# Cross attention in a decoder layer: units placed elsewhere in the order of the tensor engine, and the maximum products in pairs of 64 contraction rows

## What is computed

```
kv_r   = rope(kv_c)                                # [32, 1444, 64]
scores = q_r . k_r        over 16 heads            # 1600 query rows x 1444 keys
attn   = softmax(scores, axis=-1)
ctx_c  = attn @ kv_r                               # 64 numbers for each query row
out    = (ctx_c through w_kc_kv and Wo)            # [32, 100, 256]
x      = x + out
```

## Time and profile before

| | |
|---|---|
| median of 3 runs | 2818.99 us (2817.58 to 2822.96) |
| profiled execution, first to last instruction (span) | 2817.1 us |
| PE busy in the span | 2649.9 us (94%) |
| DVE busy | 2034.9 us (72%) |
| POOL busy | 1512.6 us (54%) |
| ACT busy | 1026.2 us (36%) |
| granted clock of PE, mean | 0.971 of full |

### The profile page before, as it was taken

The page is one execution under the profiler, slowest core; times in us unless marked ns, Lnnn a source line. Parts: engine busy times, 40 slices in busy tenths (PEclk is TensorE's granted clock), DMA queues, the critical chain, the costliest instruction groups (busy, mean ns, idle before and its releaser), DMA issues. The chain is left out here.

```text
span 2817.1 us, 40800 instructions
## 1 busy us (share of the span) xinstructions
PE 2649.9 (94%) x13650; PEld 1632.3 (58%) x13650; DVE 2034.9 (72%) x3271; ACT 1026.2 (36%) x1537; POOL 1512.6 (54%) x438
## 2 busy tenths in 40 slices
PE   6999769999979999999999999999999999999598
PEld 4545457767635555555555555555555555555388
DVE  6888758888776777677767776777677767775475
ACT  3223221111114444444444444444444444444143
POOL 1544500000026776777677767776777677767421
PEclk9999879999969999999999999999999999999799
DMA  4000031212111001100010011001100010000011
GB/s 120 19 17 23 12 107 43 47 41 47 40 41 32 21 20 25 35 20 20 25 35 20 20 25 35 20 20 25 35 20 20 25 35 20 20 20 6 25 41 41
DMA packets 56196, 88.97 MB, mean 32 GB/s; under 512 B 7146, under 2 KB 47166, under 8 KB 56016
## 3 DMA queue, kind: packets, MB, share of 16 engines
q1 hardware_dynamic: 56144, 88.29, 12.3%
HBM read 65.13 MB, written 23.14 MB: 31 GB/s over the span
## 5 line engine op out<-in xcount | busy, mean ns | idle before, releaser
L1376 POOL TENSOR_TENSOR x_acc<-x_acc,x_prob 120x1600 f32<-120x1600 f32 (+1 forms) x320 | 1157.1, 3616 | 281.7 <-ACT x_prob L1392 277.9
L1485 DVE TENSOR_REDUCE x_mx<-x_ring 124x1 f32<-124x480 f32 (+3 forms) x1248 | 784.4, 658 | 424.6 <-PE x_ring L1595 424.0
L1392 ACT ACTIVATE x_prob<-x_scores 120x800 f32<-120x800 f32 (+1 forms) x768 | 633.1, 839 | 920.2 <-PE x_scores L1542 913.4
L1554 PE MATMUL x_context<-x_prob,x_kv 120*64 120x400 f32 (+1 forms) x3072 | 653.5, 519 | 0.0
L1539 PE MATMUL x_scores<-x_qa,x_ka 128*120 128x400 f32 (+1 forms) x1536 | 552.3, 360 | 0.0
L1542 PE MATMUL x_scores<-x_qb,x_kb 128*120 128x400 f32 (+1 forms) x1536 | 530.7, 345 | 0.0
L1595 PE MATMUL x_ring<-x_ka,x_qa 128*124 128x480 f32 (+3 forms) x1248 | 516.7, 437 | 3.2 <-DVE x_mx L1485 1.1
L1595 PEld LDWEIGHTS x_ring<-x_ka,x_qa 128*124 128x124 f32 (+1 forms) x1248 | 220.0, 186 | 321.7 <-issue 161.2
L1539 PEld LDWEIGHTS x_scores<-x_qa,x_ka 128*120 128x120 f32 (+1 forms) x1536 | 280.0, 182 | 107.4 <-issue 60.6
L1554 PEld LDWEIGHTS x_context<-x_prob,x_kv 120*64 120x64 f32 (+1 forms) x3072 | 166.8, 135 | 227.0 <-issue 162.7
L1542 PEld LDWEIGHTS x_scores<-x_qb,x_kb 128*120 128x120 f32 (+1 forms) x1536 | 280.0, 182 | 26.4 <-DMA x_qb<-scratch_m 0.2
(11 more groups left out here) (165 smaller groups left out, 2867.8 us busy)
## 6 DMA issues: line engine op xcount, KB each, us to landing
x_qraw<-scratch_qp SPq DMA_DIRECT2D x64, 400.0 KB, 5.2
scratch_qp<-q_qs SPq DMA_DIRECT2D x32, 400.0 KB, 3.8
x_raw<-in_ctx SPq DMA_DIRECT2D x32, 360.0 KB
a_x<-in_x SPq DMA_DIRECT2D x8, 400.0 KB
scratch_x<-a_x SPq DMA_DIRECT2D x8, 400.0 KB
q_x<-scratch_x SPq DMA_DIRECT2D x8, 400.0 KB
x_xr<-scratch_x SPq DMA_DIRECT2D x32, 100.0 KB
scratch_x<-x_x SPq DMA_DIRECT2D x32, 100.0 KB
```

Source lines behind the costliest of these rows:

```text
L1376: pool.tensor_tensor(acc[0:rows, parity], first, prob[0:rows, c % PR], ALU.add).then_inc(acc_done.sem, 1)
L1392: act.activation(prob[0:rows, c % PR, u * HALF:(u + 1) * HALF].rearrange("p (j s) -> p j s", j=2), psc[0:rows, u, :, 0:BANK], ACT.Exp).the ...
L1485: dve.tensor_reduce(mx[0:block_rows(r), r, i:i + 1], ring[0:block_rows(r), bank, 0:b - a], AX.X, ALU.max).then_inc(rg.read[bank], 1)
L1554: mm = pe.matmul(pav[DC * s:DC * s + DC, j, 0:BANK], kv[0:rows, parity, c], prob[0:rows, c % PR, cols], start=c == 0, stop=c == LC - 1)
```

## The change

The order of the units in `side` is another one, and engines take their parts at other places:

- `kvT` goes to chunk 0 (two) and chunk 1 (one); `out` to chunk 1 behind the last score; the two `den` to the ends of chunks 4 and 5. The maxima stand in pairs behind pieces 1, 3 and 5, in chunks 2 to 9: six, six, four, four, four, four, six and five.
- Two maxima of a pair are products over 64 contraction rows each: one of partitions 0 to 63 of `qa` and `ka`, the other of partitions 64 to 127 of `qa` and `kb`. For that `kb` and `qb` keep the data that they had in their lower half in their upper half, and the row of ones or maxima is row 0. The maximum is now taken over products with the high part of the key alone.
- `den` is copied by ACT to SBUF (`save_den`); DVE takes the reciprocal from there in four halves in chunks 5 to 8 (`invert`); the products with the context (`normalise`) are one in chunk 10 and one in chunk 11.
- `rope` is taken by DVE at chunk 11 of the slot before, behind the first and ahead of the second `normalise`; ACT copies `kv_high` at the very start of the slot, ahead of the exponentials of chunk 0; DVE makes `kv_low` at the start of the slot (`split_kv`).

```diff
-        for place, u in (((1, 3), ("kvT", 0)), ((2, 0), ("kvT", 1)), ((2, 3), ("kvT", 2)), ((C_M, 2), ("mT",)),
-                         ((C_M, 3), ("den", 0)), ((C_M, 5), ("den", 1)), ((0, 4), ("out",))):
+        for place, u in (((0, 1), ("kvT", 0)), ((0, 3), ("kvT", 1)), ((1, 1), ("kvT", 2)), ((1, 3), ("out",)),
+                         ((C_M, 2), ("mT",)), ((4, 5), ("den", 0)), ((5, 5), ("den", 1))):
             side[place].append(u)
-        ticks = [(c, i) for c in range(3, C_M) for i in range(PIECES) for _ in range(1 + (ORDER[i][0] == "context"))]
-        for m in range(3 * MB):
-            side[ticks[m * len(ticks) // (3 * MB)]].append(("max", m // 3, m % 3))
+        maxima = iter([("max", m // 3, m % 3) for m in range(3 * MB)])
+        for c, at_pieces in ((2, (1, 1, 3, 3, 5, 5)), (3, (1, 1, 3, 3, 5, 5)), (4, (1, 1, 3, 3)), (5, (1, 1, 3, 3)),
+                             (6, (1, 1, 3, 3)), (7, (1, 1, 3, 3)), (8, (1, 1, 3, 3, 5, 5)), (9, (1, 1, 3, 3, 5))):
+            for i in at_pieces:
+                side[c, i].append(next(maxima))
...
-                act.copy(kb[0:DC, parity, a:b], ring[0:DC, bank, 0:b - a]).then_inc(rg.read[bank], 1)
+                act.copy(kb[DC:P, parity, a:b], ring[0:DC, bank, 0:b - a]).then_inc(rg.read[bank], 1)
+
+            def save_den(n, j):
+                wait(act, ctx_normed.sem, ctx_normed.at(n - 1, j + 1))
+                bank, value = rg.place(n, ("den", j))
+                act.wait_ge(rg.filled[bank], value)
+                act.copy(dens[:, j], ring[:, bank, 0:BANK]).then_inc(rg.read[bank], 1)
...
             def slot(n, parity, more):
+                if more:
+                    act.wait_ge(kv_roped.sem, kv_roped.at(n, 1))
+                    bank, value = rg.place(n - 1, ("kvT", 2))
+                    wait(act, rg.filled[bank], value)
+                    act.copy(ks[:, :, 0:DC].bitcast(F32R), rotated[:]).then_inc(kv_high.sem, 1)
                 for c in range(LC):
...
-                        if 2 * c + u in (3, 4, 5) and more:
-                            copy_turned(n, 1 - parity, 2 * c + u - 3)
+                        if 2 * c + u in (0, 1, 2) and more:
+                            copy_turned(n, 1 - parity, 2 * c + u)
+                        if (c, u) in ((4, 1), (5, 1)):
+                            save_den(n, c - 4)
...
+            def invert(n, j, half):
+                bank, value = rg.place(n, ("den", j))
+                dve.wait_ge(rg.read[bank], value)
+                cols = slice(half * (BANK // 2), (half + 1) * (BANK // 2))
+                dve.reciprocal(rden[:, j, cols], dens[:, j, cols]).then_inc(rden_ready.sem, 1)
...
                 for c in range(LC):
                     if c == 0 and more:
-                        rope(n, 1 - parity)
+                        split_kv(n)
                         split_q(n, 1 - parity)
...
+                    if c in (5, 6, 7, 8):
+                        invert(n, (c - 5) // 2, (c - 5) % 2)
...
+                    if c == LC - 1 and ahead:
+                        rope(n + 1, parity)
+                    if c >= LC - 2:
+                        normalise(n, c - (LC - 2))
...
+                    rows, keys = ((slice(0, DC), ka), (slice(DC, P), kb))[(3 * r + u[2]) % 2]
                     mm = pe.matmul(ring[0:block_rows(r), bank, 0:b - a],
-                                   qa[:, 1 - parity, r * MR:r * MR + block_rows(r)], ka[:, 1 - parity, a:b],
+                                   qa[rows, 1 - parity, r * MR:r * MR + block_rows(r)], keys[rows, 1 - parity, a:b],
                                    start=True, stop=True)
```

More of the change, by code:

```diff
@@ L1201, in phase_cross_attention @@
         ctxs = sb("ctxs", [P, 2, BANK])
+        dens = sb("dens", [P, 2, BANK])
         rden = sb("rden", [P, 2, BANK])
@@ L1216, in phase_cross_attention @@
         side = {(c, i): [] for c in range(LC) for i in range(PIECES)}
-        for place, u in (((1, 3), ("kvT", 0)), ((2, 0), ("kvT", 1)), ((2, 3), ("kvT", 2)), ((C_M, 2), ("mT",)),
-                         ((C_M, 3), ("den", 0)), ((C_M, 5), ("den", 1)), ((0, 4), ("out",))):
+        for place, u in (((0, 1), ("kvT", 0)), ((0, 3), ("kvT", 1)), ((1, 1), ("kvT", 2)), ((1, 3), ("out",)),
+                         ((C_M, 2), ("mT",)), ((4, 5), ("den", 0)), ((5, 5), ("den", 1))):
             side[place].append(u)
-        ticks = [(c, i) for c in range(3, C_M) for i in range(PIECES) for _ in range(1 + (ORDER[i][0] == "context"))]
-        for m in range(3 * MB):
-            side[ticks[m * len(ticks) // (3 * MB)]].append(("max", m // 3, m % 3))
+        maxima = iter([("max", m // 3, m % 3) for m in range(3 * MB)])
[3 more added lines that the diff above has]
+                side[c, i].append(next(maxima))
+        assert next(maxima, None) is None
         beside = {c: [u for i in range(PIECES) for u in side[c, i]] for c in range(LC)}
@@ L1430, in _ @@
             save_context(B)
+            for j in range(2):
+                save_den(B, j)
         @block.vector
@@ L1456, in split_q @@
                 dve.wait_ge(q_high.sem, q_high.at(n, 1))
-                dve.tensor_tensor(qb[0:DC, parity], qraw[0:DC], qa[0:DC, parity].bitcast(F32),
+                dve.tensor_tensor(qb[DC:P, parity], qraw[DC:P], qa[DC:P, parity].bitcast(F32),
                                   ALU.subtract).then_inc(q_low.sem, 1)
+            def invert(n, j, half):
[3 more added lines that the diff above has]
+                dve.reciprocal(rden[:, j, cols], dens[:, j, cols]).then_inc(rden_ready.sem, 1)
             def normalise(n, j):
-                bank, value = rg.place(n, ("den", j))
+                wait(dve, ctx_saved.sem, ctx_saved.at(n, 0))
+                dve.wait_ge(rden_ready.sem, rden_ready.at(n, 2 * j + 2))
+                bank, value = rg.place(n, ("out",))
                 dve.wait_ge(rg.filled[bank], value)
[L1464 to L1469, removed]
                 dve.tensor_tensor(ctxn[:, j], ctxs[:, j], rden[:, j], ALU.mult).then_inc(ctx_normed.sem, 1)
@@ L1486, in maximum, with slot @@
                                   ALU.max).then_inc(rg.read[bank], 1)
-            def slot(n, parity, more):
+            def slot(n, parity, more, ahead):
                 for c in range(LC):
                     if c == 0 and more:
-                        rope(n, 1 - parity)
+                        split_kv(n)
                         split_q(n, 1 - parity)
                     for u in beside[c]:
-                        if u[0] == "den":
-                            normalise(n, u[1])
-                        elif u[0] == "out":
+                        if u[0] == "out":
                             output(n, parity)
@@ L1513, in _ @@
             dve.wait_ge(memset.sem, N_MEMSET)
-            in_turn(dve, slot)
+            rope(-1, 0)
+            slot(-1, 1, True, True)
+            slot(0, 0, True, True)
+            with dve.Fori(0, (B - 4) // 2) as i:
+                for parity in (1, 0):
+                    slot(i * 2 + (2 - parity), parity, True, True)
+            slot(B - 3, 1, True, True)
+            slot(B - 2, 0, True, False)
+            slot(B - 1, 1, False, False)
             output(B, 0)
             for j in range(2):
+                for half in range(2):
+                    invert(B, j, half)
                 normalise(B, j)
```

8 lines of the change are left out of this document (5 added, 3 removed).

## The result

The changed kernel takes 3177.88 us (median of 4, 3173.59 to 3180.13) against 2818.56; the ratio is 1.1269, 95% interval 1.1253 to 1.1285. The range on record was 2900 to 3220, the time on record 3108. The profile of the changed kernel: busy times on the page, then the negated maxima, one a slot.

The account below looks back on a forecast made before the run. PE, busy 94% of the span, was taken to bound the kernel. Wait 6.5, clock 1.7 and pairs 1.4 us over 30 slots, plus 1.4 in slot 0, add 289 to 2817.1: 3108 us with 1.9 above the span; range 2900 to 3220.

Parts of the forecast that it names:

- The port: At the change of slot `rope` and `kv_low` wait for whole POOL additions; PE waits 6.5 us a slot for `kv_low`.
- Rival (b): The port doesn't hold `rope` at the change of slot: PE waits 0.6 us, 2879 us in all; chance 0.06.
- rival (a): `rope` slips in ahead of POOL at the change of slot: PE waits 3.5 us, 2981 us in all; chance 0.14.
- The pairs: Maxima in chunks 2 to 9: a pair costs one product plus shape changes, 0.42 or 0.33 us; second member waits 0.6.
- part 2: Maxima in pairs: 13.2 us a slot against 11.3, less 0.5 as `kvT` no longer waits for `out`: +1.4.
- The clock: Behind PE's wait at the change of slot, 3.5 us near half clock lose about 1.7 us a slot; bounds 0 and 3.4.
- Rival (c): `kv_low` arrives in time and pairs hide DVE's waits: 4.8 us a slot less, 2670 us, with half 2745; chance 0.10.

Follow-up runs that it names:

- Experiment 1: The changed kernel without POOL's additions of chunks 10 and 11, their signals kept: 2913.34 us, ratio 1.0334 to the kernel before.
- experiment 6: The changed kernel with the next keys made in chunk 1 of the slot before, POOL's first addition held for `kv_low`: 2904.47 us, ratio 1.0309 to the kernel before.
- experiment 5: The kernel before with `kvT`, `out`, ACT's copies and `kv_high` placed as in the change, `rope` left at the slot's start: 3077.93 us, ratio 1.0914.
- experiment 8: The changed kernel with keys made in chunk 1 of the slot before, whole maxima spread singly, whole reciprocals back in chunk 10: 2726.68 us, 0.9673 of the kernel before.
- experiment 2: The changed kernel with every maximum as one product over 128 rows, at the same places: 3111.8 us, ratio 1.104 to the kernel before.
- experiment 4: The kernel before with the maxima alone changed, to 64-row pairs behind pieces 1, 3 and 5 of chunks 3 to 9: 2864.67 us, ratio 1.0164.

## Why the prediction was right, and where it was off

**The port, right.** `rope` and `kv_low` meet POOL's last two additions, and each waits for whole ones. On record was `kv_low` 7.3 us into the slot (13.8 - 6.5); in the slot shown it came 6.7 into it (1518.34 - 1511.68). The wait was forecast at 6.5, measured at 6.0 a slot. The order in which POOL gets in was another: on record, one addition at the semaphore ahead of the sum and one behind the sum. In 20 of 30 slots both came earlier, one ahead of each instruction of L1458, and in 8 one between these two and one ahead of the sum. Two whole additions are waited for in any case, so the length came out all the same. Experiments 1 and 6 show the cause, one by taking POOL's work away, one by moving DVE's. Rival (b), that the port doesn't hold `rope`, is out by the 7.80 us of L1458 and the 4.20 of the sum; rival (a), a wait of 3.5, by waits of 5.6 us and more in every slot from 1 on. The Trainium skill's rule (SBUF — State Buffer, section Who interferes with whom) was extended rightly to instructions that had never met in the trace of before.

**The pairs, right in sign, mis-sized.** The step "a pair costs one product, 0.22, and changes of shape", 0.42 behind piece 1 and 0.33 behind pieces 3 and 5, is wrong: 0.61 and 0.41. Leaving a lone pair takes 0.41 us from its start, so its product isn't overlapped by what follows. With eight pairs behind piece 1 and eleven behind pieces 3 and 5 that would be 8 x 0.19 + 11 x 0.08 = 2.4 us a slot, and the "+1.4 us a slot" of part 2 would be 3.8. Experiment 1, with hardly a wait for `kv_low` left, has 59.25 - 56.4 = 2.85, and in that are 0.25 of such waits and up to 0.4 of half clock. So part 2 was too small by 0.8 to 1.5 us; the rest of the 2.4 didn't show, perhaps because PE waits for DVE there anyway, which no run separates. The second member waits as forecast (0.47 us behind piece 3, where 0.6 was on record).

**The clock, right in kind, too small.** 1.7 us was taken for a slot. What is left of 11.3 is 11.3 - 2.85 - 5.7 (the wait of 6.0 less the 0.25 that experiment 1 keeps) = 2.7. There was a stretch of 6.8 us at half clock behind each wait where I had one of 3.5, and in 18 of 30 slots a second one, around chunk 9, that I had not seen coming. The first costs less than half of its length: in experiment 5, which has it and not the second, about 1.4 us a slot are left for it. The second can cost 88 / 2 / 30 = 1.5 us a slot at most. By the mean clocks, time at half clock grew from 2 x 0.029 x 2817 = 163 to 2 x 0.076 x 3177 = 483 us, up to 5.3 us a slot if PE set the pace in all of it. This split of the 11.3 is by subtraction: only the wait is measured by itself.

The sum on record, 6.5 + 1.7 + 1.4 = 9.6 us a slot, stands against 5.7 + 2.7 + 2.85 = 11.3: the wait was put too long by 0.8, the other two terms too short by 2.5 together. That 3108 is only 2% below the 3178 measured owes something to these errors pointing in opposite ways.

**Rival (c)** had its point in the right place: what it needed, keys that are ready, does make a faster kernel (experiment 8), but with whole maxima and with the reciprocals out of the way, which the change does the other way round.

## What to carry to other kernels

Before work of one engine is moved, list what every other engine does in the new place, and ask which pairs of instructions exclude each other: the keys cost nothing in a stretch that POOL leaves free and 6 us a slot beside its additions. A consumer may only be moved ahead as far as its producer really gets, and what stands behind a blocked instruction in its queue is late too. One pair of half-height products between other shapes costs as much as two whole products, or more; whether several pairs in a row would pay was not tried. A long instruction of the engine that empties two banks holds up the engine that fills them: taking the half reciprocals from among the maxima won 4.7 us a slot (58.1 to 53.3, experiment 8). The fastest kernel here has whole maxima placed singly, but form and places were not varied one by one in it.

## What the runs showed of the hardware that was not expected

- Leaving a lone pair of 64-row products took 0.41 us from its start (480 columns), against 0.22 for a whole product between scores; entering it cost 0.1 us as other changes of shape do.
- When POOL's additions and DVE's instructions with two SBUF inputs were both in line, they took turns: 7.80 us for two instructions of 0.54 (one addition ahead of each), or 4.43 us for these two and 4.20 for one of 0.96, with two additions in 7.74 us. In these stretches neither engine kept the port for its next instruction.
- Around chunk 9, with PE never idle for more than half a microsecond, the granted clock was 0.54 over 7 us (1500.00 to 1507.00), and such stretches came in 18 of 30 slots. With whole maxima at the same places (experiment 2) and with pairs in the order of before (experiment 4) there was none in slots 1 to 30. What sets it off stays open.
